# A state-space scan with a mixture of experts on one core: softmax and first selection rounds two row steps further up, and the last y turned term by term into two banks

## What is computed

```
x  = layernorm input [32, 512, 256];  xn = (x - mean) / sqrt(var + eps)
# scan branch
deltaBC = xn @ W_deltaBC.T;  delta, B, C = split(deltaBC)
delta = softplus(delta @ W_dt.T + b_dt);  A = -exp(A_log)
h[t] = exp(delta*A) * h[t-1] + delta*B*xn          # 16 states a channel
y  = sum over states of h*C + D*xn
# expert branch
Sm = softmax(xn @ Wg.T) over 8 experts, swapped to [batch, expert, row]
G, I = top_k(Sm, 128)                               # per batch and expert
out = G * (gelu(xn[I] @ W1 + b1) @ W2 + b2), added back at rows I
return x + y + experts
```

## Time and profile before

| | us |
|---|---|
| median of 3 runs (2422.18 to 2428.61) | 2423.44 |
| the profiled execution | 2422.32 |
| its span in the trace | 2420.4 |
| DVE busy over the span | 2349.7 (97%) |
| PE, POOL, ACT busy | 2286.8, 2146.5, 2074.3 |

### The profile page before, as it was taken

One profiled execution on the slowest core, in us unless ns is written; L12 is line 12 of the kernel. 1 busy time (PEld: TensorE's weight loads), 2 busy tenths in 40 slices (PEclk: granted clock), 3 DMA queues, 4 the chain that ended last, 5 costly groups with the idle time before them and its releaser, 6 DMA issues. The chain is left out here.

```text
span 2420.4 us, 33772 instructions
## 1 busy us (share of the span) xinstructions
PE 2286.8 (94%) x10756; PEld 1816.4 (75%) x10756; DVE 2349.7 (97%) x1975; ACT 2074.3 (86%) x3629; POOL 2146.5 (89%) x1235
## 2 busy tenths in 40 slices
PE   7749999999999999999999999999999999999996
PEld 4437777777777777777777777777778777777775
DVE  5799999999999999999999999999999999999997
ACT  7748889898888888988888889888898989888884
POOL 5527999999999899999999999999999999999997
PEclk9969999999999999999999999999999999999998
DMA  9967575645656565555656555565646456565444
GB/s 344 338 209 266 158 221 157 177 136 148 168 147 173 145 161 141 165 154 134 184 137 173 136 166 145 141 176 143 177 127 180 127 151 163 149 173 139 128 127 79
DMA packets 151649, 403.04 MB, mean 167 GB/s; under 512 B 19536, under 2 KB 88240, under 8 KB 134832
## 3 DMA queue, kind: packets, MB, share of 16 engines
q1 hardware_dynamic: 84208, 316.72, 38.2%
q0 software_dynamic: 66048, 83.92, 20.6%
q10 hardware_dynamic: 1216, 0.23, 0.0%
HBM read 323.72 MB, written 91.75 MB: 172 GB/s over the span
## 5 line engine op out<-in xcount | busy, mean ns | idle before, releaser
L585 POOL TENSOR_TENSOR ysum<-ysum,prod 128x1024 f32<-128x1024 f32 x415 | 1121.4, 2702 | 20.3 <-DVE prod L1008 12.1
L997 DVE TENSOR_TENSOR_SCAN bank_x<-decay,bank_x 128x1024 f32<-128x1024 f32 x448 | 1024.7, 2287 | 8.9 <-DVE bank_x L936 0.5
L1163 PE MATMUL bank_l<-ext,w_sb 128*128 128x256 f32 x4096 | 968.9, 384 | 28.2 <-ACT og L757 22.6
L1229 PE MATMUL bank_l<-w_sb,hid 128*128 128x256 f32 x4096 | 939.0, 382 | 0.0
L1163 PEld LDWEIGHTS bank_l<-ext,w_sb 128*128 128x128 f32 x4096 | 760.3, 191 | 166.5 <-ACT og L757 31.0
L1229 PEld LDWEIGHTS bank_l<-w_sb,hid 128*128 128x128 f32 x4096 | 767.5, 190 | 130.0 <-issue 29.0
L717 ACT ACTIVATE decay<-delta,a_sb 128x511 f32<-128x511 f32 x1024 | 641.9, 707 | 15.8 <-POOL delta L517 14.6
L936 DVE TENSOR_TENSOR bank_x<-du,bank_b 128x1024 f32<-128x1024 f32 x512 | 617.6, 1206 | 4.7 <-ACT bank_b L748 3.2
L726 ACT ACTIVATE hid<-bank_l,b_all 128x256 f32<-128x256 f32 x1024 | 431.5, 475 | 203.8 <-PE bank_l L1163 200.7
L1008 DVE TENSOR_TENSOR prod<-bank_x,c_all 128x1024 f32<-128x1024 f32 x448 | 544.9, 1216 | 0.1
L540 POOL DMA_INDIRECT out<-og,idx_all x256 | 410.0, 1601 | 43.8 <-POOL ysum L585 42.5
(11 more groups left out here) (117 smaller groups left out, 1958.9 us busy)
## 6 DMA issues: line engine op xcount, KB each, us to landing
c_all<-bc_rows SPq DMA_DIRECT2D x128, 1024.0 KB, 5.1
b_wide<-bc_rows SPq DMA_DIRECT2D x128, 512.0 KB, 4.5
w_sb<-in_w SPq DMA_DIRECT2D x32, 1024.0 KB, 9.3
decay<-in_x SPq DMA_DIRECT2D x32, 512.0 KB, 6.8
xn_rows<-c_all SPq DMA_DIRECT2D x32, 512.0 KB, 6.5
out<-yrow POOLq DMA_DIRECT2D x32, 512.0 KB, 8.5
xr<-xn_rows SPq DMA_DIRECT2D x30, 512.0 KB, 6.0
bc_rows<-prod SPq DMA_DIRECT2D x32, 192.0 KB, 5.1
```

Of the source, the lines that this page charges most:

```text
L585: nc.gpsimd.tensor_tensor(ysum[:, m % 2], first, prod[:, i], ALU.add).then_inc(sum_done, 1)
L997: nc.vector.tensor_tensor_scan(into, decay[:, k % 2, i].rearrange("p c t -> p (c t)"), bank_x[:, s % 2], 0.0, ALU.mult, ALU.add).then_inc( ...
L1163: i = nc.tensor.matmul(bank_l[(q + v) % 2][:, (f % 2) * UT:(f % 2 + 1) * UT], w1_sb[:, e2, hc, f * P:(f + 1) * P], ext[:, v % 2, hc], star ...
L1229: i = nc.tensor.matmul(o, hid[:, w % 2, f, c * K:(c + 1) * K], w2_sb[:, w_par, f], start=False, stop=(f == FC - 1 and c == UB - 1))
```

## The change

It has two parts, and neither changes what is computed.

1. "first" and the exponential move from step 4g+9 to step 4g+7, "second" from 4g+11 to 4g+9. `TURN0` goes from 22 to 20 and ACT's copy from step 24 to 22. `EARLY` starts at step 23: one round in each of steps 23 to 31, two in each of 32 to 34, the last in 35. PE's L1064 stays in step 4g+5.
2. At the end, PE turns batch 31 term by term: `skip` for both halves, then `kept`, `ysum`, and last `prod`, each behind its own wait. The second half goes to `bank_l[0]`, which is free once the last unit's output has been read (`og_done`). POOL's last unit puts one scatter between its last two sums and one behind them.

All line numbers from here on that begin with L and stand in rows of the changed kernel are lower by one in the row stage (L885 is L886 of before).

```diff
--- before.py
+++ after.py
@@ -59,9 +59,9 @@
 ROWS = 2 * GATE
 
 WIDE = (1, 2)
-TURN0 = HALF + ROWS - 2
-EARLY = {NB - 7: (0,), NB - 6: (1,), NB - 5: (2,), NB - 4: (3,), NB - 3: (4,), NB - 2: (5,), NB - 1: (6,), NB: (7, 8),
-         NB + 1: (9, 10), NB + 2: (11, 12), NB + 3: (13, 14), NB + 4: (15,)}
+TURN0 = HALF + ROWS - 4
+EARLY = {NB - 9: (0,), NB - 8: (1,), NB - 7: (2,), NB - 6: (3,), NB - 5: (4,), NB - 4: (5,), NB - 3: (6,), NB - 2: (7,), NB - 1: (8,),
+         NB: (9, 10), NB + 1: (11, 12), NB + 2: (13, 14), NB + 3: (15,)}
 LEAD = 16
 
 
@@ -595,9 +595,8 @@
                         if i == 0 and u == NU - 1:
                             scatter(u - 1, 0)
                             scatter(u - 1, 1)
-                        if i == 2 and u == NU - 1:
-                            scatter(u, 1)
-                            scatter(u, 0)
+                        if i in (1, 2) and u == NU - 1:
+                            scatter(u, 2 - i)
                         if i == 3 and sl == 0 and there(b - 2, NB) and u < NU:
                             add_y(b - 2, u)
                         if i == 3 and sl == 2 and b == NB - 1:
@@ -632,7 +631,7 @@
             def rows(q):
                 for r in range(ROWS):
                     b = q * ROWS + r
-                    g, gq = q * 2 + r // GATE, r // GATE % 2
+                    g, gp = q * 2 + r // GATE, (r // GATE + 1) % 2
                     if b == 5:
                         act.wait_ge(params_in, 16 * 7)
                         nc.scalar.activation(a_sb[:], a_sb[:], ACT.Exp).then_inc(a_exp, 1)
@@ -667,9 +666,9 @@
                         wait(act, proj_out[(r - 3) % 4], (b - 3) // 4 * 32)
                         wait(act, lg_tr, (b - 3) // GATE)
                         nc.scalar.copy(proj[:, (r - 3) % 4], lg_banks[(r - 3) % 2][0:PJ, :]).then_inc(proj_done, 1)
-                    if r % GATE == 1 and there(g - 2, NB // GATE):
-                        act.wait_ge(lsh_done, g - 1)
-                        nc.scalar.activation(lexp[:, gq], lsh[:, gq], ACT.Exp).then_inc(lexp_done, 1)
+                    if r % GATE == 3 and there(g - 1, NB // GATE):
+                        act.wait_ge(lsh_done, g)
+                        nc.scalar.activation(lexp[:, gp], lsh[:, gp], ACT.Exp).then_inc(lexp_done, 1)
 
             through(rows, NB // ROWS)
 
@@ -877,13 +876,13 @@
                     i4 = r % 4
                     g, gp = q * 2 + r // GATE, (r // GATE + 1) % 2
                     gq = 1 - gp
-                    first = r % GATE == 1 and there(g - 2, NB // GATE)
-                    second = r % GATE == 3 and there(g - 2, NB // GATE)
+                    first = r % GATE == 3 and there(g - 1, NB // GATE)
+                    second = r % GATE == 1 and there(g - 2, NB // GATE)
                     lg = bank_t[:, 0:TC * GATE * E].rearrange("p (a e) -> p a e", e=E)
                     if first:
 
-                        dve.wait_ge(lg_tr, g - 1)
-                        nc.vector.reduce_max(lmax[:, gq], lg, axis=AX.X).then_inc(lmax_done, 1)
+                        dve.wait_ge(lg_tr, g)
+                        nc.vector.reduce_max(lmax[:, gp], lg, axis=AX.X).then_inc(lmax_done, 1)
                     if second:
 
                         dve.wait_ge(lexp_done, g - 1)
@@ -894,8 +893,8 @@
                         for c in range(TC):
                             nc.vector.bn_stats(stats[:, i4, c], xin[:, r, c]).then_inc(stats_done, 1)
                     if first:
-                        dve.wait_ge(lmax_done, g - 1)
-                        nc.vector.tensor_tensor(lsh[:, gq], lg, lmax[:, gq].unsqueeze(2).broadcast_to([P, TC * GATE, E]),
+                        dve.wait_ge(lmax_done, g)
+                        nc.vector.tensor_tensor(lsh[:, gp], lg, lmax[:, gp].unsqueeze(2).broadcast_to([P, TC * GATE, E]),
                                                 ALU.subtract).then_inc(lsh_done, 1)
                     if second:
                         dve.wait_ge(lnorm, g * 2 - 3)
@@ -1012,7 +1011,7 @@
             through(main, NJ)
             dve.wait_ge(y_tr, NB * 2)
             dve.wait_ge(y_added, (NB - 2) * 16)
-            nc.vector.tensor_copy(yrow[:, (NB - 1) % 2, 2:4], bank_x[:, 0, 0:T].rearrange("p (c d) -> p c d", c=2)).then_inc(yrow_done, 1)
+            nc.vector.tensor_copy(yrow[:, (NB - 1) % 2, 2:4], bank_l[0].rearrange("p (c d) -> p c d", c=2)).then_inc(yrow_done, 1)
 
 
         @block.tensor
@@ -1096,19 +1095,26 @@
                 pe.wait_ge(gp_prod_done, gp_prods(y * N + N))
                 pe.wait_ge(skip_done, y + 1)
 
-            def y_rows(par, half, last=False):
-
-                into = bank_x[:, 0, 0:T] if last and half else bank_t[:]
+            def y_rows(par, half):
+
                 for c in (2 * half, 2 * half + 1):
                     for dt in range(HC):
-                        part = into[:, (c % 2) * D + dt * P:(c % 2) * D + (dt + 1) * P]
+                        part = bank_t[:, (c % 2) * D + dt * P:(c % 2) * D + (dt + 1) * P]
                         rows = slice(c * P, (c + 1) * P)
-                        terms = [ysum[:, par, dt, rows], kept[:, par, dt, rows], skip[:, par, dt, rows]]
-                        if last:
-                            terms.append(prod[:, STEPS - 1, dt, rows])
-                        for t, term in enumerate(terms):
-                            o = nc.tensor.matmul(part, term, ident[:], start=(t == 0), stop=(t == len(terms) - 1), is_transpose=True)
+                        for term in (ysum, kept, skip):
+                            o = nc.tensor.matmul(part, term[:, par, dt, rows], ident[:],
+                                                 start=(term is ysum), stop=(term is skip), is_transpose=True)
                 o.then_inc(y_tr, 1)
+
+            def last_term(term, half, first=False, last=False):
+
+                into = bank_l[0] if half else bank_t[:]
+                for c in (2 * half, 2 * half + 1):
+                    for dt in range(HC):
+                        o = nc.tensor.matmul(into[:, (c % 2) * D + dt * P:(c % 2) * D + (dt + 1) * P],
+                                             term[:, dt, c * P:(c + 1) * P], ident[:],
+                                             start=(first and c % 2 == 0 and dt == 0), stop=(last and c % 2 == 1 and dt == HC - 1), is_transpose=True)
+                return o
 
             def spread_b(s, n, par):
 
@@ -1240,13 +1246,22 @@
                             if 0 < b < NB - 1 and sl == y_slot(b, 0):
                                 y_ready(b - 1)
                                 y_rows((m - 1) % 2, 0)
-                        if q in (5, 6) and u == NU:
+                        if q == 5 and u == NU:
+                            par = (NB - 1) % 2
                             pe.wait_ge(yrow_done, NB * 2 - 2)
+                            pe.wait_ge(og_done, NU * UB)
+                            pe.wait_ge(skip_done, NB)
+                            for half in range(2):
+                                last_term(skip[:, par], half, first=True)
+                            pe.wait_ge(gp_prod_done, gp_prods(NB * N))
+                            for half in range(2):
+                                last_term(kept[:, par], half)
                             pe.wait_ge(sum_done, sums(NB * N) - 1)
-                            pe.wait_ge(gp_prod_done, gp_prods(NB * N))
+                            for half in range(2):
+                                last_term(ysum[:, par], half)
                             pe.wait_ge(prod_done, dve_prods(NB * N))
-                            pe.wait_ge(skip_done, NB)
-                            y_rows((NB - 1) % 2, q - 5, True)
+                            for half in range(2):
+                                last_term(prod[:, STEPS - 1], half, last=True).then_inc(y_tr, 1)
 
             through(main, NJ)
 
```

## The result

| | before | after |
|---|---|---|
| median of 4 runs, us | 2423.74 (2422.18 to 2428.61) | 2447.14 (2446.4 to 2448.3) |
| span in the trace, us | 2420.4 | 2444.6 |
| end of the softmax (DVE's L955, now L954) | 142.19 | 160.56 |
| first and last product of the main loop (L936, now L935) | 179.27, 2399.69 | 197.42, 2425.56 |
| last product with C (L1008, now L1007) | 2404.32 | 2430.19 |

The ratio is 1.0094, 95% interval 1.0076 to 1.0111: the changed kernel is slower by 23 us, 8 us more than the 2439 forecast and inside its range.

The account below looks back on a forecast made before the run. DVE was taken to bound the main loop, the DMA engines the row stage. From the profiled 2422.3: +16.6 softmax, +1.8 clock, -2.3 end gives 2438.4; the median lies 1.1 higher, 2439.5, stated as 2439, range 2428 to 2449.

Parts of the forecast that it names:

- the ring: Row stage: L885's wait delays the shift, then ACT, PE and the next lines; 16.3 us per four batches, 19.4 with rounds.
- The clock: PE in the four plain rings: 3.5 us of idle lowers its clock, 0 to 7 us; one ring taken, +1.8.
- There is no slack to hide it: Plain rings: ACT's step (2.85 us) is as long as PE's own work, so slower PE adds 1.8 us a ring.
- The end of the softmax: DVE's L955 before: from 142.19 to 158.8, +16.6 us, with 1.8 more for PE's lowered clock.
- no limit: Last group's lines: there at about 150, DVE reaches them at about 156, so they hold nothing up.
- L915 and GpSimd's L470: Steps 17, 25, 33: a shared port lock could cost L915 up to 1.0 us each, 3 us; left out of the sum.
- The end: Behind the main loop: 16 turns left instead of 32, last sum behind a scatter; L1014 starts 2.3 us earlier.
- The main loop is as long as before.: Sign in the changed profile: second-half rounds begin about 17 us later, main loop length unchanged.
- whatever the change does before the loop shifts everything behind it, one for one: First step: DVE is busy 49.67 of 50 us from 200 us on, so earlier delays pass through the loop whole.
- The fallen clock in all rings: Rival, PE in the row stage: lowered clock in all four plain rings, 5.3 us more, 2445; chance 0.26.
- The kept pace: Rival, row stage: rows keep the DMAs' pace, only rings with rounds cost, +4.5 there, total 2426; chance 0.15.
- DVE finds its lines ready: Rival at L885: PE less than one row step behind DVE, nothing waits, 2416; chance 0.06.

Follow-up runs that it names:

- e11_behind: Changed kernel with row maxima and subtraction in the same row step, but behind DVE's shift and aggregates instead of ahead; 2423.53 us, ratio 1.0.
- e7_scatter_last: Changed kernel with both of the last unit's scatters behind POOL's last sum; one run, 2446.13 us.
- e1_tail: Kernel before with only the new end: last y turned term by term, last scatters in the new order; 2421.6 us, ratio 0.9986.

## Why the prediction was right or wrong

- **Where it waits, and the ring.** Right, piece by piece. L885 starts at 49.15, 66.16, 83.70, 100.99, 120.14 and 139.29 where the prediction had 48.0, 64.3, 81.8, 98.7, 118.1 and 137.5. `e11_behind` shows the reason itself: what counts is the shift queued behind the waiting instruction.
- **The size of the ring.** 16.3 plain (and what ACT's copies add) and 19.4 with rounds were 17.0 and 19.15. In the ring quoted above 0.54 us of that is the clock.
- **The clock.** The mechanism was right and happened in all rings, as that rival had it: L1043 after 3.58 us of idle took 1.97. But a plain ring paid at most 0.6 us for it and not 1.8: ACT's wait for L1053 was 0.54, 0.60, none and 0.39 us in the four, since ACT, one batch behind, had work of its own meanwhile. "There is no slack to hide it" was the wrong step. That the sum came out is luck.
- **The end of the softmax.** Forecast 16.6 + 1.8 = +18.4, measured +18.37, closer than its parts deserve: the first ring began 0.5 us late (32.20), the four plain rings together took 1.8 more than the 67.0 without the clock, and the two with rounds 0.5 less than 38.8. The last lines came at 154.4 instead of 150, and DVE was there at 157.8 and did not wait; no limit, as said.
- **L915 and GpSimd's L470.** Rightly left out: in the steps where both fall, L470 runs at 72.16 to 73.32 and L915 starts at 73.54 (0.25 us); in the next, 108.50 and 110.80 (0.26); in the third, 144.96 and 148.49 (0.29). The lock itself showed again, on shifts: the one at 72.93 in the changed kernel took 0.40 us and ended with L470, and in `e11_behind` L899 began at 63.12 beside L470's 63.06 (1.16) and took 1.12 us. That is the earlier trace rows once more. The rule of the Trainium skill (SBUF — State Buffer, SBUF: two separate sides), that the later one waits for the whole of the other, agrees with all three.
- **The end.** Forecast -2.3, measured -2.37; the 16 turns took 3.7 us where the sum had 3.4. The price of the scatter, 1.3, is what `e7_scatter_last` gave back.
- **"The main loop is as long as before."** Wrong, by 7.7 us, and this is nearly the whole difference between 2439 and 2447. The range had no term for it. The step that failed is the first one: "whatever the change does before the loop shifts everything behind it, one for one". That held for DVE's own instructions alone. SyncE's copies followed the last batch's way through the rows, which ended 23 us later against DVE's 18, and so they fell on the loads of the loop's first units. I had followed what the moved rounds free on DVE, and not what these rounds had covered: the stores, copies and gathers on their way to the loop.
- **The rivals.** The fallen clock in all rings (2445) came nearest in time for a reason that holds only in part. The kept pace is what `e11_behind` makes true, and there the time is indeed that of before. That DVE finds its lines ready occurred in none of the first seven places.

Open is the +0.70 us behind the last copy. From the last add to the end of the span the kernels with the new end take 7.7 to 8.0 us, those with the old one 7.3 (before), 7.6 and 7.75; whether it belongs to the new end no run tells.

## What to carry to other kernels

When an instruction that waits is moved up, price what stands behind it in its queue, and who waits for that: the same wait, with what followed from it, cost 23 us ahead of the shift and nothing a few instructions further back. A shift of a whole phase is one for one only if every queue shifts by the same amount, so compare the starts of the DMA queue with those of the engine and not the engine's alone. Bulk copies that nobody waits for soon should not stand behind a wait that ends just when the next phase begins to load: here the DMA share was 0.01 from 190 to 200 us, just ahead of them, and bringing them forward made the changed kernel's loop 9.8 us shorter (and the loop of the kernel before, with the new end, some 3 us).

## What the runs showed that I had not expected

- The issue of one DMA can take long by itself. Not the load right behind the four copies (0.61 us) but the next load of `c_all` (1 MB, L397), issued 14.6 us behind them, held SyncE's queue for 11.35 us (6.03 before, 8.7 in `e1_tail` and `e11_behind`). It took 0.34 us in each of the six kernels in which the copies were left out or came some 30 us earlier. What stands behind it in the queue waits along: the next issue is at 229.46. Why the issue takes so long no run tells.
- The clock of TensorE after 3.6 us of idle: eight turns in 1.97 us and the next four matmuls in 2.65 instead of 1.09 and 1.88 to 1.94, back at the full level with the turns at 39.98 (1.04). Something like it happened behind each of the seven waits, and a long idle of one engine can still be nearly free where the next engine has a batch in hand. The idle just before is not all that counts: at 18.65 the changed kernel's turns took 1.97 us after 2.20 us of idle, where those of the earlier trace rows took 1.09 after 2.45.
